# Rows of the two edge stages read from eight copies in HBM, sixteen partitions from each

## What is computed

```
xp = (x @ W).reshape(n, HEADS, C)
alpha = leaky_relu(a_src[src] + a_dst[dst] + a_edge, 0.2)
m = segment_max(alpha, dst)
ea = exp(alpha - m[dst])
den = segment_sum(ea, dst)
msg = xp[src] * (ea / (den[dst] + 1e-16))[:, :, None]
out = segment_sum(msg, dst)

x = x + L0_gnn(layernorm(x), src, dst)
x = x + L0_ffn(layernorm(x))
x = x + L1_gnn(layernorm(x), src, dst, edge_attr)
x = x + L1_ffn(layernorm(x))
```

## Time and profile before

| | |
|---|---|
| median of 3 runs | 7070.55 us |
| lowest and highest run | 7054.83 and 7079.41 us |
| span of the profiled execution, first to last instruction | 7097.3 us |
| TensorE, VectorE, ScalarE, GpSimd busy | 69, 56, 37, 43% of the span |
| moved by DMA | 840.43 MB, 604088 packets, 118 GB/s |
| projection (q_) | about 670 to 1059 us |
| first edge stage (b_) | about 1059 to 2480 us |
| second edge stage (w_) | about 4477 to 5900 us |

### The profile page before, as it was taken

The page is one execution under the profiler, slowest core; times in us unless marked ns, Lnnn a source line. Parts: engine busy times, 40 slices in busy tenths (PEclk is TensorE's granted clock), DMA queues, the critical chain, the costliest instruction groups (busy, mean ns, idle before and its releaser), DMA issues. The chain is left out here.

```text
span 7097.3 us, 86053 instructions
## 1 busy us (share of the span) xinstructions
PE 4867.8 (69%) x21453; PEld 3463.5 (49%) x21454; DVE 3992.7 (56%) x9527; ACT 2611.2 (37%) x4956; POOL 3068.5 (43%) x3260
## 2 busy tenths in 40 slices
PE   4368475777777788377877733355555556999999
PEld 3246134556556578345555433243444444666565
DVE  4248135999999976311221297466666666445443
ACT  0134003555555533033333331355555553222222
POOL 2641605666666657366666400466666661000000
PEclk6568697998998965588988856677777777999999
DMA  1001147888888876333333215555555552000000
GB/s 50 1 0 29 44 156 235 246 248 248 248 246 247 246 181 168 91 84 83 81 80 80 76 58 185 157 145 145 146 147 146 146 147 83 11 10 10 10 10 11
DMA packets 604088, 840.43 MB, mean 118 GB/s; under 512 B 209556, under 2 KB 406907, under 8 KB 603453
## 3 DMA queue, kind: packets, MB, share of 16 engines
q0 software_dynamic: 159136, 383.90, 20.6%
q1 hardware_dynamic: 306877, 405.04, 17.8%
q10 hardware_dynamic: 137972, 50.36, 3.0%
HBM read 687.43 MB, written 158.32 MB: 119 GB/s over the span
## 5 line engine op out<-in xcount | busy, mean ns | idle before, releaser
L1372 POOL DMA_INDIRECT b_got<-tmp_l_table,b_src x928 | 877.4, 946 | 542.9 <-issue 250.9
L2471 POOL DMA_INDIRECT w_got<-tmp_l_table,w_src x928 | 879.8, 948 | 531.0 <-issue 254.3
L2720 PE MATMUL w_pa<-w_got,w_hot 128*128 128x264 f32 x1856 | 662.5, 517 | 312.1 <-DVE w_got L2627 195.8
L3202 POOL DMA_INDIRECT t_got<-tmp_f_table,t_src x672 | 634.2, 944 | 410.1 <-DVE t_sums L3280 203.8
L1616 PE MATMUL b_pk<-b_keys,b_hot_t 128*128 x1856 | 552.5, 450 | 283.1 <-issue 201.7
L2720 PEld LDWEIGHTS w_pa<-w_got,w_hot 128*128 128x128 f32 x1856 | 448.8, 254 | 433.1 <-issue 330.3
L1616 PEld LDWEIGHTS b_pk<-b_keys,b_hot_t 128*128 128x128 f32 x1856 | 386.6, 218 | 376.2 <-issue 316.7
L3653 DVE SCALAR_TENSOR_TENSOR l_accs<-l_po,l_prob,l_accs 128x256 f32 (+1 forms) x392 | 173.6, 480 | 564.5 <-PE l_po L3762 564.5
L1631 PE MATMUL b_pa<-b_got,b_hot 128*128 128x260 f32 x1856 | 483.8, 407 | 9.0 <-DVE b_acc L1543 5.0
L3324 PE MATMUL t_po<-t_w,t_hid 128*128 128x256 f32 x1568 | 410.2, 409 | 116.2 <-issue 82.6
L3705 ACT ACTIVATE l_h<-l_ph,l_bn 128x896 f32<-128x896 f32 x224 | 245.1, 1097 | 653.3 <-PE l_ph L3752 653.3
(11 more groups left out here) (577 smaller groups left out, 9716.2 us busy)
## 6 DMA issues: line engine op xcount, KB each, us to landing
tmp_g_acc<-b_acc SPq DMA_DIRECT2D x232, 260.0 KB
w_spread<-tmp_g_rel_rows SPq DMA_DIRECT2D x232, 256.0 KB
t_spread<-tmp_f_rel_rows SPq DMA_DIRECT2D x174, 256.0 KB
b_spread<-tmp_g_rel_rows SPq DMA_DIRECT2D x116, 256.0 KB
e_attr<-in_edge_attr ACTq DMA_DIRECT2D x103, 256.0 KB
tmp_f_experts<-t_y SPq DMA_DIRECT2D x28, 896.0 KB
yl_y<-tmp_f_experts SPq DMA_DIRECT2D x20, 896.0 KB, 11.1
b_got<-tmp_l_table,b_src POOLq DMA_INDIRECT x928
```

The source lines that it names most:

```text
L1372: pool.indirect_dma_start(out=got[:, m % NB, u, :], out_offset=None, in_=T["l0_table"], in_offset=bass.IndirectOffsetOnAxis(ap=src[:, m * ...
L2471: pool.indirect_dma_start(out=got[:, p % 3, u, :], out_offset=None, in_=T["l1_table"], in_offset=bass.IndirectOffsetOnAxis(ap=src[:, p * R ...
L2720: mm = pe.matmul(pa[:, (k * RS + n) % SUMS, 0:WV], hot[:, (k * B4 + b) % 3, u - b * U, :], got[:, k, u, 0:WV], start=(u == 2 * n), stop=(u ...
L3202: pool.indirect_dma_start(out=got[:, g % RING, u, :], out_offset=None, in_=T["f_table"], in_offset=bass.IndirectOffsetOnAxis(ap=src[:, g * ...
```

## The change

After the last table, `GraphTables.sync` stores the rows of rel eight times more in each of the two types, each time into its own part of two new tensors in HBM, `g_spread` (f32) and `g_spread16` (bf16). One part is 1024 rows of 128 values and 17 rows more that are left empty, so that the parts begin 1041 rows apart. These are 16 stores, 8 of 512 KB and 8 of 256 KB, on SyncE, before the loop over the chunks. The wait at the stage's end counts them (128 + 32 x 8).

Both edge stages read the spread rows from there. The source of a load was one row with a step of 0 over 128 partitions. It is now a pattern of three dimensions, 8 copies, 16 partitions with a step of 0, and the values; the destination is as before. The number of these loads, their bytes and the waits before them are the same. The spread rows of the stage between the two (t_ names, another list of edges) are not touched.

```diff
+COPIES = 8
+
+def spread_of(ap, start, n):
+
+    flat = ap.rearrange("c s e -> c (s e)")[:, bass.ds(start, n)]
+    return flat.unsqueeze(1).broadcast_to((COPIES, P // COPIES, n))
...
             sp.dma_start(T[L.name + "_last"], self.last[:, :]).then_inc(self.stored, 16)
+        for c in range(COPIES):
+            for name, of in (("_spread16", self.rel16), ("_spread", self.rel)):
+                sp.dma_start(T[L.name + name][c, 0:L.blocks * P, :].rearrange("(b s) e -> s b e", s=P), of[:, :, :]).then_inc(self.stored, 16)
...
-            sp.wait_ge(tables_of.stored, 128)
+            sp.wait_ge(tables_of.stored, 128 + 32 * COPIES)
...
-        rel_flat = T[L.name + "_rel_rows16"].rearrange("s e -> (s e)")
+        rel_rows = T[L.name + "_spread16"]
...
-                sp.dma_start(spread[:, h, :, :], rel_flat[bass.ds(half * (R // 2 * P), R // 2 * P)].rearrange("(b e) -> b e", b=B4 // 2)
-                             .partition_broadcast(P)).then_inc(spread_in[h], 16)
+                sp.dma_start(spread[:, h, :, :].rearrange("p b e -> p (b e)"), spread_of(rel_rows, half * (R // 2 * P), R // 2 * P)
+                             ).then_inc(spread_in[h], 16)
...
-        rel_flat = T[L.name + "_rel_rows"].rearrange("s e -> (s e)")
+        rel_rows = T[L.name + "_spread"]
...
-                    sp.dma_start(spread[:, b, :], rel_flat[bass.ds((p * B4 + b) * (U * P), U * P)].partition_broadcast(P)
+                    sp.dma_start(spread[:, b, :], spread_of(rel_rows, (p * B4 + b) * (U * P), U * P)
                                  ).then_inc(spread_in[b], 16)
...
+    shapes.update({"g_spread": ([COPIES, GRAPH.blocks * P + 17, P], F32), "g_spread16": ([COPIES, GRAPH.blocks * P + 17, P], BF16)})
```

## The result

The changed kernel takes **7143.23 us** (median of four runs, 7127.22 to 7157.92), the kernel before 7072.59 (four runs, 7054.83 to 7079.41). The ratio is 1.0089, with a 95% interval of 1.0073 to 1.0104: 63 us slower, 52 to 74. The change costs three times the 20 us of the sum.

The account below looks back on a forecast made before the run. VectorE was taken to bound the first edge stage, no engine being full in the second. Terms of +15 (stores), +3 (stage heads), +2 (first edge stage) and 0 made +20 us on the median 7070.55: 7090 us, range 7062 to 7150.

Parts of the forecast that it names:

- VectorE sets the pace: First edge stage: VectorE, 182.99 of 200 us busy, bounds it, and the DMA engines, 0.82 busy, follow.
- 8 engines: Spread loads: with 8 copies as slowest dimension, a load could run on 8 DMA engines; the sum should stand with 8 or 16.
- +2 us in the first edge stage: Spread loads land later; usual rounds lose nothing, a few tight ones up to 2.5 us; between 0 and +60.
- Rival 1: First edge stage: loads on 8 engines land after ScalarE wants them; 1 us in each of 58 rounds, 7149 us; chance 0.20.
- 0 us for SyncE's issues with three dimensions: Both edge stages: issues take a few tenths more, but SyncE waits for ScalarE or VectorE each round, so 0 us.
- 0 us in the second stage: Second edge stage: a transfer has nearly a whole round of slack (119 waits of SyncE for the buffer), so 0 us.
- +3 us at the heads of the stages: Heads of both edge stages: first rows are waited for; two to four loads on half the engines cost 0.7 us more each.
- +15 us for the stores: Projection: 16 stores delay x of the second chunk by 23 to 39 us, partly absorbed; +15 us, range 5 to 35.
- price one: Projection: the 16 stores priced by their packets at 22.6 ns each on 16 engines, 23 us.
- price two: Projection: the 16 stores priced by SyncE's own time, 4.87 us a pair, by 8, 39 us.
- rival 2: Projection: the slow stretch takes the whole delay of the stores; +5 us in all, 7076 us; chance 0.17.
- Rival 3: Both edge stages: reads of one shared row hold up the gathers, so copies make it faster; -48 us, 7023 us; chance 0.08.

Follow-up runs that it names:

- E7: Kernel before, with VectorE weighing only 32 of the 65 values of each head in the first edge stage; ratio 0.9996, -3 us.
- E8: Kernel before, its single row read as 4 x 32 x values (4 DMA engines) in the first edge stage only; ratio 1.0047, +33 us.
- F1: Kernel before, only the load of the second half of a round's spread rows in the first edge stage written as 8 x 16 x values; ratio 1.0027, +19 us.
- E3: Kernel before, its single row read as 8 x 16 x values (8 engines) in both edge stages, no stores or copies; ratio 1.0072, +51 us.
- E4: Kernel before, its single row read as 16 x 8 x values (three dimensions, 16 engines) in both edge stages; ratio 1.0047, +33 us.
- E2: Changed kernel with the loads of the kernel before, so only the 16 stores are left of the change; ratio 1.0014, +10 us.
- F2: Kernel before, only the load of the first half of a round's spread rows in the first edge stage written as 8 x 16 x values; ratio 1.0024, +17 us.
- E5: Kernel of E3, with the second half's spread load issued right behind the first, ahead of the store, in the first edge stage; ratio 1.0050, +35 us.

## Why the prediction held in its range and missed in its size

- **"VectorE sets the pace"** is the step that failed, and the main one. It was read from 183 busy us in 200, and from waits that add up to little. E7 took 2.2 us a round from VectorE and got nothing. The profile had a sign of it: in 47 of 50 rounds the first sum waited, 0.53 us on the mean and never under 0.4. An engine that sets the pace would hardly wait at one place in nearly every round. I had taken the 15.3 us of the earlier trace rows for the only wait that mattered, and left out the row behind it, of 14.8 us for TensorE's products, which belongs to the same place.
- **8 engines.** That the loads could run on 8 was read rightly from the 36 closing packets of the earlier trace rows; the count of q1 shows it to the packet.
- **+2 us in the first edge stage** is the term that was mis-sized: it measured 33. It was worked out from when the load lands and what stands behind it on ScalarE, with 4.0 us in hand. By E8 and F1 that is not how it acts. Rival 1's 1 us a round was as far above the 0.5 that came as the forecast's nothing was below, and its mechanism was the wrong one too: no row of E3 shows ScalarE waiting for the landing, and where one does (E8) the price is no higher.
- **0 us for SyncE's issues with three dimensions.** The few tenths more that were expected are there, 333 to 557 ns in the second stage. The form is not free: 15 us in the first stage and 18 in the second. That SyncE has time was true (in 4700 to 5700 us it still waits 399.8 us for ScalarE in E4, 442.3 before) and did not help.
- **0 us in the second stage**: 18. The forecast said itself that it would be wrong altogether if this stage moved. The slack of the transfer (119 waits of SyncE for the buffer) was read rightly, and it hides the landing; the price came by another way.
- **+3 us at the heads of the stages**: no run measures this alone. In the traces ScalarE's first use of the spread rows in the second stage comes 16.5 us after the first issue before and 19.5 after, but 18.2 in E2, with the old loads; in the first stage 5.7 and 5.2.
- **+15 us for the stores**: 10, 4 to 16. The norm began at 746.67, a little ahead of the 750 to 766, for the 16 stores took 26.42 us of SyncE, between price one (23) and price two (39). The delay was partly absorbed, as worked out. The 5 us of rival 2 are inside the interval as well.
- **Rival 3** is refuted as far as 12 us can be told: eight copies on 16 engines are not measurably faster than one row on 16. The 83 ns of a packet said so.
- **The chances and the range**: slower by over 0.3% had 0.47, the largest. The price of a load's form had none in the list, only "0 us". The median lies 7 us under the upper end of the range, and that end was set by rival 1, whose mechanism did not occur: that the range held is luck.

**What stays open.** How a load of another form makes TensorE's counts come later is not shown. The longer pause follows two spread loads on SyncE, the other none, and it grew with each load that was changed (F1, F2); that fits with something that SyncE's issues and GpSimd's share, but no run tests it. In the second stage TensorE's counts are late too (382 of 564 recorded in 4700 to 5700 us of the kernel before, and none of 1025 by VectorE and ScalarE), but whether another form makes them later there is not shown. Why part of the price went away when both loads stood next to each other (E5) is open as well, and so is why 4 engines cost no more than 8.

## What to carry to other kernels

An engine that is 92% busy may still follow others: look for a small wait that comes at the same place in nearly every round, and for engines that go on together, and test by making the busy engine's work lighter before you call it the one that sets the pace. That busy and idle time of some other engine add up to the round is no proof that this one does. The source pattern of a load, its dimensions and the size of the slowest, is part of its price even if bytes, packets and waits stay the same and its landing has slack: keep a broadcast from one row as two dimensions with 128 as the slowest, and measure before paying for copies, which gave nothing here.

## What the runs showed of the hardware that I had not expected

- While GpSimd issues indirect DMAs back to back (0.945 us each and 0.305 between), waits for TensorE end late, and those for VectorE and ScalarE do not (444 of 623 counts, and none of 837). In the first edge stage ScalarE, VectorE and GpSimd go on within 0.4 us of each other, about 2 us after the last of 8 gathers. With VectorE relieved, its sum still began 2.05 us after the modelled end of the products it needs. The 44.35 us wait of the earlier trace rows for a tile of TensorE, among scatters back to back, looks like the same thing; that was not tested.
- 128 partitions that read one row of 2 KB cost no more than 16 that read each of eight copies (33 us against 28, and 12 us is what can be told).
- A load with three dimensions in its source costs 15 us in 116 loads (0.13 us each, give or take 12 us in all) and 18 us in 232 (0.08 us each, give or take 8) of the whole kernel's time, by nothing but its form.
- Between traces of kernels with the same projection, the first gather of the edge stage stood anywhere from 1044.8 to 1063.9 us, and the median of the kernel before differed by 52 us between chips: only ratios taken on one chip can tell 20 us in this kernel.
